# Moving the turns and output matmuls of a fused attention and FFN kernel into the PSUM banks of the second pass

## What is computed

```python
qk = (x @ Wqk_w.T + Wqk_b).reshape(b, n, H, E, 2)      # H = 8 heads of E = 8
q, k = qk[..., 0], qk[..., 1];  v = (x @ Wv_w.T + Wv_b).reshape(b, n, H, E)
attn = softmax(q @ k.T) / sqrt(64)                      # per head, 1024 x 1024
x = layernorm(x + (attn @ v).reshape(b, n, 64) @ Wo_w.T + Wo_b)
g = silu(x @ Wg.T) * (x @ Wu.T)                         # 512 -> 1792, int4 weights, scales per group of 128
x = layernorm(x + g @ Wd.T)                             # 1792 -> 512
```

## Time and profile before

| what | us |
|---|---|
| three timed executions | 577.76, 577.70, 572.97 |
| their median | 577.7 |
| the profiled execution, its own time | 574.47 |
| its span, first to last instruction | 572.7 |

### The profile page before, as it was taken

How to read it: one execution, slowest core, us unless ns; L and a number is a source line. 1 busy time by engine, 2 the same in 40 slices (tenths; PEclk the granted TensorE clock), 3 DMA queues, 4 the chain that set the end, 5 groups by cost and what they waited for, 6 DMA issues and landing times.

```text
span 572.7 us, 7463 instructions
## 1 busy us (share of the span) xinstructions
PE 526.8 (92%) x2640; PEld 197.5 (34%) x2640; DVE 416.4 (73%) x697; ACT 408.4 (71%) x587; POOL 226.6 (40%) x284
## 2 busy tenths in 40 slices
PE   8897888789798989889999999999999999999992
PEld 3222112122121212214444445444454444544441
DVE  3589888877986888006787879776687667787666
ACT  1531877677676778797787877878778787787881
POOL 8020700012392100303756656663235733338442
PEclk9999699899998989899999999999999999999997
DMA  5595690004002200000212211010000010000101
GB/s 174 160 194 108 170 144 2 2 4 145 1 2 54 21 3 0 2 1 1 38 37 19 57 20 37 19 73 1 1 2 1 8 67 0 2 1 2 73 1 73
DMA packets 28933, 24.59 MB, mean 43 GB/s; under 512 B 19072, under 2 KB 21248, under 8 KB 28896
## 3 DMA queue, kind: packets, MB, share of 16 engines
q1 hardware_dynamic: 25472, 18.08, 12.2%
q0 software_dynamic: 3424, 6.03, 6.2%
HBM read 20.08 MB, written 4.19 MB: 42 GB/s over the span
## 4 chain that ended last, share of the span: by engine, by line
PE 74%; DVE 17%; ACT 4%; DMA 2%; issue 2%; POOL 1%; SPq 0%; POOLq 0%; ACTq 0%; DVEq 0%
PE ps L890 17%; PE ps L902 17%; PE ps L919 16%; DVE mxh L1019 14%; PE ps L841 7%; PE ps L771 5%; PE ps L805 3%; PE ps L709 3%; PE ps L826 2%; ACT pbuf L589 2%; PE ps L756 1%; DMA stack<-mrows 1%; PE ps L928 1%; PE ps L715 1%; DMA arena<-xT 1%
## 5 line engine op out<-in xcount | busy, mean ns | idle before, releaser
L1019 DVE TENSOR_REDUCE mxh<-ps 128x1 f32<-128x512 f32 x256 | 163.6, 684 | 33.5 <-PE ps L771 32.1
L1121 DVE TENSOR_SCALAR ps<-ps,ratio 128x512 f32<-128x512 f32 x168 | 121.7, 754 | 72.4 <-PE ps L902 71.8
L589 ACT ACTIVATE pbuf<-ps,gamma 128x1024 f32<-128x1024 f32 x128 | 135.4, 1116 | 48.1 <-PE ps L826 48.0
L655 ACT ACTIVATE ps<-ps,ratio 128x512 f32<-128x512 f32 x168 | 106.2, 657 | 41.5 <-PE ps L890 41.5
L919 PE MATMUL ps<-stack,wd 128*128 128x512 f16 x448 | 129.5, 379 | 0.6 <-POOL stack L515 0.6
L890 PE MATMUL ps<-arena,wg 128*128 128x512 f16 x448 | 115.3, 379 | 0.1
L902 PE MATMUL ps<-arena,wu 128*128 128x512 f16 x448 | 115.3, 379 | 0.0
L676 ACT ACTIVATE ps<-ps,ratio 128x512 f32<-128x512 f32 x156 | 102.8, 665 | 16.2 <-PE ps L919 16.2
L771 PE MATMUL ps<-stack 64*128 64x512 f16 x256 | 87.6, 404 | 9.6 <-DVE mxh L1019 4.9
L513 POOL CAST stack<-pbuf 128x512 f16<-128x512 f32 x56 | 34.2, 611 | 113.7 <-DVE pbuf L1128 113.7
L841 PE MATMUL ps<-pbuf,arena 128*32 128x512 f32 x512 | 73.2, 646 | 0.6 <-ACT pbuf L589 0.6
(11 more groups left out here) (102 smaller groups left out, 353.4 us busy)
## 6 DMA issues: line engine op xcount, KB each, us to landing
arena<-xT SPq DMA_DIRECT2D x16, 256.0 KB, 5.6
x<-x SPq DMA_DIRECT2D x2, 2048.0 KB, 9.2
out<-x SPq DMA_DIRECT2D x3, 1024.0 KB, 4.2
wg<-gq POOLq DMA_DIRECT2D x4, 448.0 KB, 10.2
wu<-uq POOLq DMA_DIRECT2D x4, 448.0 KB, 12.4
wd<-dq POOLq DMA_DIRECT2D x2, 896.0 KB, 13.3
out<-x SPq DMA_DIRECT2D x4, 256.0 KB, 2.4
wqk_s<-wqkT SPq DMA_DIRECT2D x1, 256.0 KB, 2.7
```

The costliest lines, as they stand in the source:

```text
L589: nc.scalar.activation(pbuf[:, pi % 4, :].rearrange("p (a n) -> p a n", a=2), ps[:, 2 * (pi % 2):2 * (pi % 2) + 2, :], ACT.Exp, scale=gamm ...
L655: nc.scalar.activation(gbank[t % 2], gbank[t % 2], ACT.Copy, scale=gr[:, t % G, c:c + 1])\
L1019: nc.vector.tensor_reduce(mxh[:, f % 2, qh, half:half + 1], ring_bank("first", n, 0), AX.X, ALU.max)\
L1121: nc.vector.tensor_scalar(ubank[t % 2], ubank[t % 2], ur[:, t % G, c:c + 1], None, ALU.mult)\
```

## The change

- M (for `f` of 1 and more), avT, attT and wo leave the ring of three banks. They are called turns now and take a place in the order of the second-pass bank pairs: `shared` is the order of all `scores(n, pair)` and turns, and the entry i uses banks 0 and 1 or banks 2 and 3 by `i % 2`. An entry waits for the reader of the entry i - 2, whatever it is. M of `f = 0`, which comes before step 0, stays in the ring.
- A step on PE is now: `scores(n, 0)`, two first-pass matmuls, `scores(n, 1)`, two first-pass matmuls, at most one turn, `av(n - 1)`. `AHEAD` is 46.
- attT is two transposes instead of four: each turns the 64 columns of two token tiles at once, so the tiles of a pair lie in partitions 0 to 63 and 64 to 127. wo is two uses instead of four, in steps 16u + 19 and 16u + 20: each is two fp32 matmuls over 64 rows, one in each row half, into two banks, and ACT copies both banks to `wob` with one instruction.
- The bias no longer goes through the matmul. It is loaded to `wob[:, 0, :]` (a DMA of 256 KB on SP after `wo_s`, which itself grows from 96 to 128 rows), and POOL adds it to each half of `x` with one instruction of 128 x 4096 elements (`add_bias`), after `split_max(1)` and `split_max(2)`.
- SP: the load of `x` for batch 1 goes ahead of `max_rows(2)` and `max_rows(3)`.
- DVE: `scale_ratios` runs after step 56 instead of step 16. The memsets of `att` go.
- The last turns of the tail are in the FFN's periods 0 (avT, attT) and 1 (two wo).

The core of the diff:

```diff
-AHEAD = FG + 12
+AHEAD = FG + 14
...
-        def ring_at(n):
...
-            return first[0:2] + other + first[2:4]
-        WO_AT = (4, 6, 7, 8)
+        def firsts_at(n, pair):
+            m = AHEAD + 4 * n + 2 * pair
+            return range(m, min(m + 2, FIRST))
+        before = [("first", n) for n in range(AHEAD)]
+        before.insert(FG + 6, ("M", 0))
...
+        def turns_at(n, pair):
+            if pair == 0:
+                return []
             f, r = divmod(n + 3, KT)
             if r == 0 and f < NB * NG:
-                other.append(("M", f, 0))
+                return [("M", f, 0)]
...
+        WO_AT = (3, 4)
+        tail = [("avT", NB * NG - 1, 0), ("attT", NB - 1, 0), ("wo", NB - 1, 0), ("wo", NB - 1, 1)]
+        def in_shared_banks():
+            order = []
+            for n in range(ALL):
+                for pair in range(2):
+                    order += [("scores", n, pair)] + turns_at(n, pair)
+            return order + tail
+        def shared_banks(*use):
+            return 2 * (shared_index[use] % 2)
+        def wait_shared_read(engine, kind, n, k):
+            if kind == "scores":
+                engine.wait_ge(s_exp, 2 * n + k + 1)
+            elif kind == "avT":
+                engine.wait_ge(s_norm, n + 1)
+            else:
+                engine.wait_ge(s_read, out_count[kind, n, k])
...
+            sp.dma_start(wob[:, 0, :], bo).then_inc(s_bo, 16)
...
             sp.dma_start(x1[:, 8:16, :], x[8:16].rearrange("t p n -> p t n")).then_inc(s_x[1], 16)
+            max_rows(2)
+            max_rows(3)
...
+            def add_bias(b):
+                pool.wait_ge(s_bo, 16)
+                pool.wait_ge(s_x[b], 16)
+                half = x1[:, b * N // P:(b + 1) * N // P, :]
+                nc.gpsimd.tensor_tensor(half, half, wob[:, 0:1, :].to_broadcast([P, N // P, D]), ALU.add)\
+                  .then_inc(s_xb, 1)
...
             for n in range(ALL):
-                exps(n)
-                if n and n % KT == 0:
-                    av_out(n // KT - 1)
-                for use in ring_at(n):
-                    ring_use(*use)
+                for pair in range(2):
+                    exps(n, pair)
+                    if pair and n and n % KT == 0:
+                        av_out(n // KT - 1)
+                    for use in turns_at(n, pair):
+                        turn_out(*use)
...
+            def turn(kind, u, k):
+                i = shared_index[kind, u, k]
+                wait_shared_read(pe, *shared[i - 2])
+                at = shared_banks(kind, u, k)
+                dst = bank[at]
...
-                    for t in range(BT):
-                        mm = nc.tensor.transpose(dst[0:KR, t * P:(t + 1) * P], att[:, t, :], ident[:])
+                    for t in range(0, BT, 2):
+                        mm = nc.tensor.transpose(dst[:, t * HD:(t + 2) * HD],
+                                                 att[:, t:t + 2, :].rearrange("p t n -> p (t n)"), ident[:])
...
-                    mm = nc.tensor.matmul(dst, attT[:, k * P:(k + 1) * P], wo_s[:], start=True, stop=True)
-                mm.then_inc(s_rf, 1)
+                    for j in range(2):
+                        rows = slice(j * HD, (j + 1) * HD)
+                        mm = nc.tensor.matmul(bank[at + j], attT[rows, k * P:(k + 1) * P], wo_s[rows, :],
+                                              start=True, stop=True)
+                mm.then_inc(s_of, 1)
...
             for n in range(ALL):
-                uses = ring_at(n)
-                late = max(1, len(uses) - (2 if len(uses) >= 4 else 0))
-                scores(n, 0)
-                for use in uses[0:1]:
-                    ring_use(*use)
-                scores(n, 1)
-                for use in uses[1:late + 1]:
-                    ring_use(*use)
+                for pair in range(2):
+                    scores(n, pair)
+                    for m in firsts_at(n, pair):
+                        ring_use("first", m)
+                    for use in turns_at(n, pair):
+                        turn(*use)
                 if n:
                     av(n - 1)
-                for use in uses[late + 1:]:
-                    ring_use(*use)
...
-                if n == STEPS:
+                if n == ALL - KT:
                     scale_ratios()
```

More of the change, by code:

```diff
@@ L33 @@
 KT = N // P
-KR = 96
 TH = H // 2
@@ L208, in build @@
         block = ctx.enter_context(nc.Block())
-        def ring_at(n):
-            first = [("first", AHEAD + 4 * n + j, 0) for j in range(4) if AHEAD + 4 * n + j < FIRST]
-            other = []
+        def firsts_at(n, pair):
[3 more added lines that the diff above has]
+        before.insert(FG + 6, ("M", 0))
+        ring_order = before + [("first", n) for n in range(AHEAD, FIRST)]
+        ring_index = {use: i for i, use in enumerate(ring_order)}
@@ L218, in ring_at @@
             f, r = divmod(n - 9, KT)
-            if r == 0 and 0 <= f:
-                other.append(("avT", f, 0))
+            if r == 0 and f >= 0:
+                return [("avT", f, 0)]
             u, r = divmod(n - STEPS, STEPS)
[L222 to L226, removed]
-            return first[0:2] + other + first[2:4]
-        WO_AT = (4, 6, 7, 8)
@@ L231, in build @@
[L231 to L244, removed]
@@ L246, in ring_count @@
-        def ring_count(*use):
-            return ring_index[use] + 1
[L250 to L264, removed]
+            if 0 <= u < NB - 1 and r == 2:
+                return [("attT", u, 0)]
@@ new lines, in build @@
+        shared_index = {use: i for i, use in enumerate(shared)}
+        all_turns = [use for use in shared if use[0] != "scores"]
+        turn_count = {use: i + 1 for i, use in enumerate(all_turns)}
+        out_count = {use: i + 1 for i, use in enumerate(use for use in all_turns if use[0] != "avT")}
+        def shared_banks(*use):
[5 more added lines that the diff above has]
+                engine.wait_ge(s_norm, n + 1)
+            else:
+                engine.wait_ge(s_read, out_count[kind, n, k])
@@ L295, in slots_of_periods @@
             slots, turns, t = {}, {}, 0
-            ring = {0: [[tail[0]], [], [tail[1]], []], 1: [[use] for use in tail[2:6]]}
+            last = {0: [[], [tail[0]], [], [tail[1]]], 1: [[], [tail[2]], [], [tail[3]]]}
             for p in range(2 * TILES):
-                slots[p] = [[("ring", *use) for use in uses] for uses in ring.get(p, [[]] * C)]
+                slots[p] = [[("tail", *use) for use in uses] for uses in last.get(p, [[]] * C)]
                 if p < HELD or len(turns) == NB:
@@ L679, in slot @@
                 for what, *args in slots[p][k]:
-                    if what == "ring":
-                        ring_use(*args)
+                    if what == "tail":
+                        turn_out(*args)
                     if what == "down" and down_by_act(args[1]):
@@ L933, in slot @@
                 for what, *args in slots[p][k]:
-                    if what == "ring":
-                        ring_use(*args)
+                    if what == "tail":
+                        turn(*args)
                     elif what == "down":
@@ L1103, in _ @@
             for n in range(ALL):
-                for use in ring_at(n):
-                    ring_use(*use)
+                for pair in range(2):
+                    for m in firsts_at(n, pair):
+                        first(m)
+                    for kind, f, _ in turns_at(n, pair):
+                        if kind == "avT":
+                            normalise(f)
                 if n == 0:
@@ L1154, in slot @@
                 for what, *args in slots[p][k]:
-                    if what == "ring":
-                        ring_use(*args)
+                    if what == "tail":
+                        if args[0] == "avT":
+                            normalise(args[1])
                     elif what == "down" and not down_by_act(args[1]):
```

180 lines of the change are left out of this document (101 added, 79 removed).

## The result

The changed kernel takes 559.5 us (median of four executions, 558.77 to 572.26), the one before beside it 577.7. The ratio is 0.971, with a 95% interval from 0.963 to 0.978. The forecast was 560 us. Some executions take some 12 us more, the profiled ones of e5, e8 and e9 among them, which show PE at half clock from 21 to 48 us, during the projections; they stay out of the ratios, and of those three profiles only the lengths from step 3 on are read.

What follows compares the result with a forecast made beforehand. A loop of latencies through PE and DVE over three banks bounds each step, no engine full. Stretches +1.7 - 8.0 - 4.9 - 3.0 and tail -1.5 give -15.7, so 558.8, plus 1.7 for timed executions: 560 us, range 550 to 572.

Steps and rivals of the forecast that it cites:

- The plain step: Step without a turn: a loop of reduce, weights, av, scores pair and f0 takes 2.70 us, 0.21 longer; bounds 2.48 to 2.81.
- Rival 3: Plain steps: f0 need not wait behind the scores pair, steps stay at 2.48, 10 us less, 549 us; chance 0.08.
- The turns: Steps with a turn between f3 and av: M 2.88 us, avT 3.41, attT 3.00, wo 3.70.
- The guess on wo: wo's two fp32 row halves run side by side, 1.05 us for two tiles; extra 1.00 per step, bounds 0.8 and 2.1.
- The second such change of a turn: Second tiling-mode drain before av in avT, attT and M: 2 to 3 us over 17 turns, left out of the sum.
- Rival 1: Second-pass steps: PE idle drops the clock to half, a step takes about 4.1, at most 4.5 us; chance 0.08.
- Rival 2: The 23 turns each add an exp and wo's halves run one after the other: 577 us, no change; chance 0.12.
- The stretches: Steps 0, 16, 32, 48 to 63: 50.2 us (+1.7), 49.3 (-8.0), 47.3 (-4.9), 37.9 (-3.0).
- the wait for the maxima: At step 8 the DMA of the maxima comes last: steps ready at 82.0 us, maxima land at about 83.5.
- The statistics: Second stretch: four of 0.6 us with aggregation, 3.3 us of DVE time, 1.3 hidden by two steps, 2.0 added.
- The bias adds: On POOL, two adds of 10 us each during the second pass, costed at nothing.
- The tail: In the FFN: two of four 0.86 us output matmuls and two transposes less on PE, about -1.5 us.

Runs made afterwards that it cites:

- e5: Changed kernel with the second token tile's matmul of each wo pair left out; wo steps took 3.65 us, against 3.66 with both tiles.
- e8: e6 with POOL's two loads of the down weights issued after the first bias add; its two shortest executions took 552.27 and 551.67 us.
- e9: Changed kernel with the two bias adds on POOL cut from 128 x 4096 elements to 8; shortest execution 560.32 us.
- e1: Changed kernel with the first-pass matmuls in the former order, one behind av, and turns still in the second-pass banks; 560.45 us.
- e11: Changed kernel with the scale ratios moved back behind step 16; 563.2 us, 3.8 above the changed kernel run again.
- e6: e1 with the division ahead of its step's fourth reduce on DVE, and M, attT and the last avT behind av on PE; 555.4 us.
- e2: Kernel before with only PE's order changed: two first-pass matmuls behind each scores pair, av last, turns still in the old ring; 570.8 us, ratio 0.990.
- e3: Kernel before with only the scale ratios moved behind step 56; 569.05 us, ratio 0.988.
- e10: Kernel before with the edits of e2 and e3 together, turns and four single wo still in the ring of three; 567.3 us, ratio 0.984.

## Why the prediction was right, and where it was off

**The plain step: right.** 2.70 forecast, 2.70 measured, by the loop that was written down (the chain above). It is the step on which most hung, since 9 of the 16 steps from 32 to 48 are plain and all others stand on it. Rival 3, the shorter loop, falls with it; e1, which takes the scores pair out of the loop, gives the 2.49 that this loop gives without it.

**The turns: right.** Forecast and measured: M 2.88 and 2.87, avT 3.41 and 3.37, attT 3.00 and 3.07, wo 3.70 and 3.66. The guess on wo, side by side, had no row; e5 shows it. On the change between halves and whole rows: `av` starts 0.32 us after a plain step's f3, M starts 0.32 after f3 (98.61 and 98.93), but wo, which keeps to the row halves, 0.21 (116.03 and 116.24). The Trainium skill (TensorEngine Tiling (Array Packing), Key Properties) says that a change of tiling mode drains the engine, and the trace agrees with 0.1 us for it. The second such change of a turn, before `av`, which by that rule would have made 2 to 3 us for all turns, is not seen: M adds 0.17 to a step in all, and `av` starts 0.16 after it.

**Rival 1, the clock: fell.** PE is idle for 25.8 of the 173.6 us from 67 to 241, over 0.4 us a step, and its granted clock stays at full, 2.4 GHz, all the while. (By its own terms a step at half clock would have been at most 2.70 + 1.93 = 4.63 us, not 4.5; none came.) The page of the Trainium skill that was weighed (TensorE: Matmul & The Clock Gate, A second HAM failure mode: psum-queue depth-cycling) tells of short idles between matmul groups that make the clock swing; no step of this trace shows that. Most falls that the runs do show from step 3 on stand behind one long stall: PE was idle 1.5 to 2.5 us before each of the five of the kernel before, and 2.6 in e11. But the rival had taken rows 10 for a condition, and the runs do not bear that out. In the kernel before PE was just as little busy, 1.84 of 3.40 us, from 95.5 to 98.9 around the M of the earlier trace rows, and in the changed kernel 1.77 of 3.40 us from 140.4 to 143.8, with 1.62 idle in one piece behind the statistics, and no fall followed. In e6 the clock fell at 142.8 though no idle time in the 8 us before it was over 0.80 us. What decides a fall stays open.

**Rival 2, the turns cost what they saved: fell for this kernel**, but its mechanism is real and showed where the order was tightened. In the changed kernel avT waits for an exp: its weights load 0.41 us behind f3's (109.58 and 109.99), where M's load 0.32 behind. That is 0.09 for the exp, where 0.12 had been counted. In e1 the same wait is 0.56, and `scores` waits 1.55 for the turn's reader.

**The stretches.** Forecast 50.2, 49.3, 47.3 and 37.9, measured 48.6, 49.2, 47.2 and 38.9. The first ends at 105.5 and not at 106.0, 1.2 us later than before and not 1.7. As forecast, step 8 waits for the maxima; it started at 83.0 and not at 83.5, and from there the stretch took 22.5 us (21.6 before), as forecast. The part up to step 8 took 26.1 us (26.9 before). It began 1.15 us later (56.94, before 55.79), which was not forecast, but the wait for the maxima ended only 0.3 later than before, so the stretch grew by 0.1 and not by 1.7. In the fourth the forecast was 1 us short. Between first exps two of its steps were 0.6 over each: 57, forecast 2.6, took 3.23, and 52, forecast 3.1, took 3.66; the others together were 0.2 under. The timeline of the changed kernel around step 57:

```profile
227.50 0.63 ACT L625 ACTIVATE avt<-ps 128x512 f32<-128x512 f32 x1
227.98 2.17 ACT L618 ACTIVATE pbuf<-ps,gamma 128x1024 f32<-128x1024 f32 x2
229.19 0.42 PEld L839 LDWEIGHTS ps<-ident,avt 128*128 128x128 f32 x4 [1.40 <-ACT pbuf L618]
...
230.77 0.12 PEld L875 LDWEIGHTS ps<-stack 64*128 64x128 f16 x4 [0.84 <-ACT pbuf L618]
```

"avT 2.6 (the next scores now wait for the second exp)" left out that `av` stands behind avT on PE. avT waits 1.40 us for an exp that itself stands behind the copy of bank 6; `av` and the next scores follow both. e6, which puts this avT behind `av`, brings the step to 2.65. Step 52 had been priced by ACT alone (2.05 + 1.0); measured, it is as long as a whole wo step, though two of its reduces are missing.

**The statistics: right** in size. Steps 25 to 27 took 2.0 us more than steps 41 to 43, which hold no statistics; 2.0 had been forecast. **The bias adds: right** to cost nothing (e9). One took 8.88 us and not 10.

**The tail: too large.** -1.5 forecast, -0.6 measured (317.0 against 317.6). PE's busy time from 240.72 to 260.50 is 17.9 us, where it was 19.1 before, 1.2 less. But before, the chain that ended last ran through PE from 259.8 to 270.8 with 0.03 us of gap; its first and last pieces of that, in the kernel before:

```profile
259.80 0.43 PE ps L902 x2
...
269.51 0.86 PE ps L902 x4
270.37 0.45 PE ps L890 x2
```

Now DVE and ACT are in it. The same chain of the changed kernel:

```profile
246.45 0.29 DVE att L1083
246.74 1.19 DVE st L1088 x2
...
249.26 1.08 PE ps L852 x4
...
250.36 0.98 ACT wob L648
...
251.96 1.28 ACT L701
```

PE is idle 1.84 us from 240.72 to 260.50, and was 1.29 in the same part before. So about half of the saved work went into waits for DVE and ACT.

**The total.** Forecast -15.7 against the profiled execution; it was -14.4. The 1.3 us between them (1.2 by the spans) are the fourth stretch with 1.0 and the tail with 0.9, less 0.5 in the first and 0.1 in each of the other two. But the medians are 18.2 apart. The rest lies in the kernel before: at 574.47 its profiled execution was faster than most of its timed ones. Its time follows its mean clock: 570.05 us at 0.981, 571.8 at 0.976, 576 at 0.968, 577 to 579 at 0.961 to 0.964. Where the clock fell in those, no profile tells. The three shorter executions of the changed kernel had 0.985 to 0.988 and lie within 1.3 us. So it is in part luck that the forecast hit 559.5 so closely: the sum was 1.3 us too good, and 1.7 had been added for timed executions, which the changed kernel did not need.

**Where the gain comes from**, by e2, e3, e10, e11 and the table: the ratios out of the loop 3.1 us (e2 to e10) to 4.7 (e3), and 4.3 in the changed kernel (e11); the new order 3.3 (e3 to e10) to 4.9 (e2), by shorter turn steps and a clock that stays up, in spite of 0.21 in each plain step; the turns out of the ring and the outputs side by side 7.0 (e10 to the changed kernel), which no run divides between the two.

## What to carry to other kernels

When two engines pass a few banks around, write the loop down (reader, free bank, matmul, what PE must do before the next of that bank) and count what stands in it: the step is that sum and no engine's busy time, and anything else that takes a place in the ring costs a loop. Before pricing an order of instructions, count how many steps are really plain, and look at the turn steps first: here the order that was 0.21 us better in a plain step gained nothing until the division and the turns were moved too. A stall costs more than its own length where the clock falls with it (3.04 and then 6.8 at half clock in e11), so look at the granted clock behind each long wait.

## What the runs showed of the hardware that was not expected

- The clock is part of the time of each execution, not only of a stretch: 570 us at a mean of 0.981 to 579 at 0.961, for one kernel on the same inputs.
- Two fp32 matmuls of 64 rows and 512 columns in different row halves cost what one does: steps of 3.66 and 3.65 us with two and with one.
- The small DMA of the maxima took 5.7 us in the chain beside large loads of another queue, and no longer ended a wait once those were moved (step 7 from 4.01 to 2.49).
- One add of 128x4096 on POOL took 8.88 us, where eight of 128x512 took 1.27 each, 10.1 together:

```profile
L521 POOL TENSOR_TENSOR x<-x,wob 128x4096 f32<-128x4096 f32 x2 | 17.8, 8875 | 0.0
```
